# Four small ScalarE operations of the second scan phase issued in other slots

## The reference

```python
xz = jnp.einsum('bhwc,ec->bhwe', x, in_w)
xa, z = jnp.split(xz, 2, axis=-1)
xc = silu(dwconv3x3(xa, conv_w, conv_b))
xs = ...                       # xc in 4 directions: rows, columns, and both reversed
delta = softplus(dts + dt_b)   # dts, Bs, Cs are projections of xs
dA = jnp.exp(delta * A);  dBu = delta * Bs * xs
h = a * h + bu                 # a scan over the 4096 positions, 8 states per channel
y = sum_n(h * C) + Ds * xs     # and ysum adds the 4 directions
yo = layernorm(ysum, ln_g, ln_b) * silu(z)
out = jnp.einsum('bhwd,cd->bhwc', yo, out_w)
```

## Time and profile before

| | |
|---|---|
| median of 3 runs | 7420.16 us (7418.65 to 7431.59) |
| profiled execution | 7393.42 us, span 7391.3 us |
| granted TensorE clock over the span | 0.895 |
| busy in the span | VectorE 86%, TensorE 82%, ScalarE 74%, GpSimd 74% |
| passes 8 to 39 | about 3462 to 4943 us |
| passes 40 to 55 | about 4943 to 5694 us |
| passes 56 to 63 | about 5694 to 6062 us |

### The profile page before, as it was taken

The page is one execution under the profiler, slowest core; times in us unless marked ns, Lnnn a source line. Parts: engine busy times, 40 slices in busy tenths (PEclk is TensorE's granted clock), DMA queues, the critical chain, the costliest instruction groups (busy, mean ns, idle before and its releaser), DMA issues. The chain is left out here.

```text
span 7391.3 us, 105881 instructions
## 1 busy us (share of the span) xinstructions
PE 6028.6 (82%) x18336; PEld 2105.4 (28%) x18336; DVE 6340.8 (86%) x7490; ACT 5467.9 (74%) x11128; POOL 5454.8 (74%) x4289
## 2 busy tenths in 40 slices
PE   7888888888888883688888888888888778798696
PEld 2222222222222221222222222222222113497252
DVE  6999999999999997299999999999999985533636
ACT  7888888888888883477888888888888863222757
POOL 5888888988888883289999999999999971000706
PEclk8898999999898986788899999999999888997898
DMA  4444544544454444488888888888888863346312
GB/s 101 110 103 112 116 105 106 119 109 103 111 113 109 103 113 118 114 190 192 193 192 193 191 192 191 193 193 197 195 193 195 192 151 102 126 142 191 86 50 79
DMA packets 584349, 1050.60 MB, mean 142 GB/s; under 512 B 105735, under 2 KB 140732, under 8 KB 579100
## 3 DMA queue, kind: packets, MB, share of 16 engines
q1 hardware_dynamic: 584060, 1047.70, 59.9%
HBM read 857.89 MB, written 189.54 MB: 142 GB/s over the span
## 5 line engine op out<-in xcount | busy, mean ns | idle before, releaser
L1648 POOL TENSOR_TENSOR scan_prod<-scan_hs,scan_BC_rep 128x512 f32<-128x512 f32 x1536 | 1931.8, 1270 | 197.5 <-DVE scan_hs L1572 193.7
L664 POOL TENSOR_TENSOR mamba_prod<-mamba_hs,mamba_BC_rep 128x512 f32<-128x512 f32 x1536 | 1916.7, 1271 | 215.6 <-DVE mamba_hs L621 213.6
L621 DVE TENSOR_TENSOR_SCAN mamba_hs<-mamba_dA,mamba_carry,mamba_dbx 128x512 f32<-128x512 f32 x1152 | 1425.7, 1265 | 1.6
L1417 ACT ACTIVATE scan_dA<-scan_delta_rep,scan_a_neg 128x512 f32<-128x512 f32 x1536 | 1094.2, 713 | 274.1 <-DVE scan_hs L1572 266.3
L1193 PE MATMUL scan_u_rep<-scan_du,scan_sel 96*128 96x512 f32 x1536 | 895.9, 669 | 396.2 <-DVE scan_hs L1572 395.4
L546 ACT ACTIVATE mamba_dA<-mamba_delta_rep,mamba_a_neg 128x512 f32<-128x512 f32 x1536 | 1092.5, 712 | 118.6 <-DVE mamba_hs L621 115.8
L1572 DVE TENSOR_TENSOR_SCAN scan_hs<-scan_dA,scan_carry,scan_dbx_even 128x512 f32<-128x512 f32 x768 | 972.0, 1266 | 40.4 <-ACT scan_carry L1397 33.7
L1572 DVE TENSOR_TENSOR_SCAN scan_hs<-scan_dA,scan_carry,scan_u_rep 128x512 f32<-128x512 f32 x768 | 972.2, 1266 | 0.1
L600 DVE TENSOR_TENSOR mamba_dbx<-mamba_u_rep,mamba_BC_rep 128x512 f32<-128x512 f32 x1152 | 777.4, 675 | 85.2 <-PE mamba_u_rep L332 72.4
L1971 POOL TENSOR_TENSOR ffn_sq<-ffn_xm 96x512 f32<-96x512 f32 x64 | 66.2, 1034 | 956.0 <-DVE ffn_xm L1939 946.3
L332 PE MATMUL mamba_u_rep<-mamba_du,mamba_sel 96*128 96x512 f32 x768 | 465.2, 690 | 319.0 <-DVE mamba_hs L621 318.5
(11 more groups left out here) (286 smaller groups left out, 10545.8 us busy)
## 6 DMA issues: line engine op xcount, KB each, us to landing
scan_BC_rep<-proj_rows SPq DMA_DIRECT2D x1024, 256.0 KB, 6.4
scan_delta_rep<-proj_rows SPq DMA_DIRECT2D x1024, 192.0 KB, 3.6
mamba_BC_rep<-bc_units SPq DMA_DIRECT2D x512, 256.0 KB, 8.0
mamba_delta_rep<-delta_units SPq DMA_DIRECT2D x512, 192.0 KB, 3.6
proj_rows<-scan_dbc SPq DMA_DIRECT2D x256, 224.0 KB, 7.1
delta_units<-mamba_delta SPq DMA_DIRECT2D x128, 192.0 KB, 5.4
by_n<-fin_res SPq DMA_DIRECT2D x32, 768.0 KB, 3.2
fmid_src<-by_n SPq DMA_DIRECT2D x32, 768.0 KB, 5.3
```

The lines of the kernel that those rows point to most:

```text
L621: nc.vector.tensor_tensor_scan(hs[:, s % RING_H], dA[:, s % RING_A], dbx_bank(s)[:], carry[:, bass.ds(at, 1)], op0=ALU.mult, op1=ALU.add). ...
L664: pool.tensor_tensor(prod[:, (G * u + s) % RING_P], hs[:, s % RING_H], BC_rep[:, u, QUADS + s % QUADS], ALU.mult).then_inc(s_prod, 1)
L1417: nc.scalar.activation(dA[:, (2 * k + s) % 4], delta_rep[:, k, s // 2], ACT.Exp, scale=a_neg[lay][:, at:at + 1]).then_inc(s_dA, 1)
L1648: pool.tensor_tensor(prod[:, (G * k + s) % RING_P], hs[:, (G * k + s) % RING_H], BC_rep[:, k, 2 + s % 2], ALU.mult).then_inc(s_prod, 1)
```

## The change

Three operations of ScalarE get another slot. In a slot they stand behind the group's exponential and carry copy. `start_y` goes from slot 23 to 17, ahead of that slot's `softplus_end`, and keeps its waits. The affine pass goes from 22 to 21, so it stands ahead of the exponential of slot 22. The copy of z goes from slot 3 to 4, behind one more exponential and ahead of the softplus operations. Nothing is added or removed, and the order on the other engines is the same.

```diff
-                        if has_out and at == 3:
+                        if has_out and at == 4:
                             copy_z(f)
...
-                        if has_conv and at == 23:
+                        if has_conv and at == 17:
                             if has_out:
                                 act.wait_ge(s_mean, f + 1)
                             start_y(conv, n + CH, at_xc)
...
-                        if has_out and at == 22:
+                        if has_out and at == 21:
                             affine(f, out)
```

## The result

| | before | after |
|---|---|---|
| median of all runs beside each other | 7421.26 us (7415.30 to 7431.59, 15 runs) | 7436.64 us (7430.74 to 7446.97, 15 runs) |
| ratio after to before | | 1.0023, 95% interval 1.0016 to 1.0030 |
| profiled execution, span | 7391.3 us | 7429.5 us |

Three operations moved, not the four of the title. The change makes the kernel slower by 0.23%, 17 us (the two medians lie 15 us apart). The largest term of the forecast, the six passes with a late mean, came out near its size (about 14 us for 10). The 7 us for the ordinary passes of layer a did not come, since the store queue, which the forecast took for a serial cost, hides a late store.

A forecast was written before the change was run, and what follows sets the result against it. Layer a was taken as bound by SyncE's serial store queue, layer b's pass end by the eviction waiting on the residual tile; 7 + 10 + 3 = 20 us on 7420 gave 7440 us, range 7415 to 7472 (forecast's own 7432 to 7452).

The forecast's parts named there:

- the six passes with a late mean: Last tile of an image: late mean delays the scans of slot 18 and next slot 0; 10 us, bounds 0 and 17.
- the ordinary passes of layer a: Late slot 22 sum delays SyncE's store: 0.25 us for each of 28 passes, 7 us, bounds 0 and 28.
- Slot 17: Write of Y waits 1.7 us for the mean ahead of the exponential of slot 18, which starts 2.5 us later.
- The step of 1.07 us from an exponential to its scan: Time from an exponential's start to its scan's earliest start; stalls worked out with it may be 0.36 us too long.
- Hidden, with 0.17 us to spare: Pass 26, layer a: the scan of slot 18 can start at 4328.70 and started at 4328.87, so no stall.
- The steps behind it: Slots 18 to 23: variance and normalisation about 1.0 us later; exponential of 18 to that of next slot 0, 11.7 us.
- One ordinary pass of layer a has no stall: Pass 26: four exponentials in a row catch up by the next slot 0; no VectorE stall, margin 0.1 us.
- What is late at the store stays late, since that queue is serial: SyncE's store queue, layer a: delay of the slot 22 sum beyond its slack counts, 0 to 0.8 us a pass.
- every lag reaches the store queue: Rival, chance 0.14: GpSimd's 1.0 us counts in each of 28 passes, plus 17 and 13 us: +58 us, 7478.
- all hidden: Rival, chance 0.28: store queue and residual load set the end, ScalarE's lag vanishes into existing VectorE waits: -5 to +12 us, 7424.
- The ordinary passes of layer b: Stalls in slots 18 and 23 fall before the existing residual-tile wait: 3 us for 14 passes, between 0 and 13.
- The rule of occupancy: Rank engines by occupancy, work on the highest first: reordering ScalarE, at 74%, changes nothing, sum 0.

The follow-up runs named there:

- the kernel with the wait alone: Kernel before, plus a ScalarE wait for the mean in slot 17 ahead of the softplus, write of Y left in slot 23: 7409.08 us, ratio 1.0000.
- the second profile of before: The kernel before, unchanged, run and profiled once more: profiled span 7422.2 us, median 7428.00 us, ratio 1.0009 to the kernel before.

## Why the prediction came out right, point by point

- **Slot 17.** The write waits 48 times, 1.73 us in ordinary passes (1.7 forecast) and 3.01 to 5.94 us in the six. From the end of the mean to the exponential of 18 it is 4341.48 - 4339.55 = 1.93 us (1.92 forecast), and to its scan 1.00 us (1.07). All steps of this sum held. The step of 1.07 us from an exponential to its scan was named as a sign of being wrong if a scan came sooner, and scans do: 1.00 us in ordinary passes and 0.74 in pass 31, where the scan waits for the exponential and not for the carry copy. The forecast had allowed for up to 0.36 us less. Layer b's stall of 0.34 us in each ordinary pass was forecast as 0.4.
- **"Hidden, with 0.17 us to spare"** in layer a was wrong: 0.34 us late in most passes. The cover counted on in the earlier trace rows held a wait for a load. In pass 26 of before VectorE waited 0.49 us for one just ahead of the scan of 17:

```profile
4325.90 0.70 DVE L1528 TENSOR_TENSOR scan_dbx_even<-scan_u_rep,scan_BC_rep 128x512 f32<-128x512 f32 x1 [0.49 <-DMA scan_BC_rep<-proj_rows]
```

  The mean starts ahead of that wait, so the wait gave the mean, and ScalarE, 0.6 us more time. In the changed kernel such waits are gone (3.0 us of stalls in place of 40.0), and the cover with them: the scan of 18 can come 2.60 us behind the end of the mean, not the 3.20 us of before.
- **The steps behind it.** From the exponential of 18 to that of the next slot 0 it takes 4354.17 - 4341.48 = 12.7 us, not 11.7. The missing microsecond is the variance: TensorE idle for the late square and then at 1.2 GHz, so the affine pass waits longer in its turn. "One ordinary pass of layer a has no stall" was wrong by four stalls. In the kernel with the wait alone, where the ordinary passes have no stall at slot 18, they have none at 22 either, and 12.7 us at 23 in 28 passes, no more than before.
- **"What is late at the store stays late, since that queue is serial"** was the step that failed outright, and with it the term of 7 us. The store lands behind the loads before it; a store that leaves up to some 5 us later lands at the same time. SyncE's wait for GpSimd rose from 0.5 to 165.4 us in 800 us, "several us" being far too little, and the wait for landings fell by 161 us.
- **The ordinary passes of layer a: 7 us forecast, none measured** (1309.4 us for the 28 passes, 1311.1 in the second profile of before). In return for stalls of its own ScalarE took away the waits for loads (40.0 to 3.0 us over the layer). The rivals "every lag reaches the store queue" and "all hidden" were each half right: every lag reached the queue, and in the ordinary passes the queue hid it.
- **The last tile of an image: 10 us forecast, 14 measured**, within the bounds of 0 and 17. Here the mechanism was as forecast: the late mean holds ScalarE, and the scan of 18 waits. That stall was 1.43 to 4.55 us, 2.35 on the mean of the six, with 2.1 forecast for pass 31, where it was 1.50. The loss was 1.5 us a pass in the four of layer a, near the 1.6 that the forecast took for each, and 3.9 us in passes 47 and 55 of layer b.
- **The ordinary passes of layer b: 3 us forecast, 3 measured** (668.1 against 665.2 us), but with no more than the number right: other profiles without an added wait have 657.5 to 668.0. The forecast let the wait for the residual tile absorb the lag of slot 23. The chain overran it: over the whole layer 38.0 us of stall at slot 24 became 21.0, but 28 us of new stalls came in slots 18 to 23, and 1.31 us at slot 24 in pass 46 are ScalarE's chain with the residual matmul in it, not the tile.
- **The copy of z** at nothing: right, ratio 1.0001 alone. **The affine pass**: its wait is there and costs nothing alone.
- **The sum** of 20 us against 17 measured: 7 + 10 + 3 forecast, about -2 + 14 + 3 by the pair of profiles. The term for the store queue was too large by more than the six passes were too small, and the closeness of the sum is in part luck; the spread of the profiles does not let the terms be had more exactly.
- **The rule of occupancy**, as the forecast took it, gave 0. By the Trainium skill, page Perfetto Trace Analysis, section Identifying the Most-Contended Engine, the engine with the highest occupancy is the one to optimize first, and ScalarE at 74% was not that engine; a reordering on it still cost 0.23%. The other estimate, from the Trainium skill's page DMA: Bandwidth & Descriptors, section Anatomy of one DMA, some 2.5 us for the store, was set aside for the 6.8 us of the trace. That section gives its figure for DMAs of the GpSimd path, and this store is SyncE's. What the trace of the changed kernel shows is still near it: a store that leaves over 5 us after the loads is followed by the next loads after 2.4 us (shortest 2.24), and the one that left when all loads had landed, 8.07 us after them, took 2.33 us. Most of the 6.8 us were time behind the loads, not the store's own.

## What to carry to other kernels

Before a wait is put ahead of an operation in an in-order queue, look for work of the same slot that can stand ahead of the wait: here 1.2 us of softplus on the other side of it separated 1.0003 from 1.0023. Price the wait first in the passes where what it waits for is late: six of 48 passes carried nearly all of the cost here. A margin read from one pass of a trace is only good if the pass holds no wait of another cause; work it out from the engines' own pace. And where a queue waits for a store that stands behind its own loads, that wait is slack for whoever fills the store, not a serial cost.

## What the runs showed of the hardware

- TensorE idle for 1.55 us, busy for 1.13 and idle for 1.29 again (the clock fell within this last stretch) ran the two 96 x 512 fp32 matmuls of the variance at the 1.2 GHz level (granted 0.50). With one idle stretch of 2.16 us and 1.12 us of work behind it, as before in pass 26, it ran them at 2.4 GHz (granted 1.00). Over all pairs the median of one was 1061 in place of 592 ns, and 641 ns with two extra matmuls ahead of them.
- A store of 224 KB took from 2.24 us (issued over 5 us after the loads) to some 7.3 us (issued within 1 us), lateness and duration together being 8.05 us on the mean. It never landed before the loads issued ahead of it.
- Two profiled executions of one kernel lay 31 us (0.4%) apart. Of this 18 us sat in layer a, 46.26 against 46.82 us a pass, most of it as waits for loads. Half a microsecond a pass in layer a can't be read from one pair of profiles.
